# One key tile per head from GpSimd to VectorE, and the row maxima turned by TensorE into ScalarE's hands, in a decoder layer's two attentions

## The reference

```python
x = layernorm(x + self_attention(x))          # 16 heads of 32; ALiBi bias, even heads look back, odd heads ahead
x = layernorm(x + cross_attention(x, context, mask))   # 16 heads of 32; mask[b, 0, q, k] == 0 gives -1e9
x = layernorm(x + feed_forward(x))            # quantised gate/up/down, inner width 1536
# attention, per head: softmax(q @ k.T / sqrt(32) + bias) @ v
```

## Time and profile before

| | us |
|---|---|
| median of three runs | 3442.01 |
| the profiled execution | 3449.42 |
| its span in the trace | 3447.6 |

### The profile page before, as it was taken

The page is one execution under the profiler, slowest core; times in us unless marked ns, Lnnn a source line. Parts: engine busy times, 40 slices in busy tenths (PEclk is TensorE's granted clock), DMA queues, the critical chain, the costliest instruction groups (busy, mean ns, idle before and its releaser), DMA issues. The chain is left out here.

```text
span 3447.6 us, 79793 instructions
## 1 busy us (share of the span) xinstructions
PE 2725.7 (79%) x24128; PEld 1463.9 (42%) x24128; DVE 2539.6 (74%) x4873; ACT 1712.4 (50%) x3083; POOL 2054.8 (60%) x1542
## 2 busy tenths in 40 slices
PE   6888568888886777999999999950999899500999
PEld 3444235555553432555555555530444333200444
DVE  7777667777775666888888888848334599795776
ACT  2344247666664223656665666530233466575433
POOL 2344479898987215999999999973200366532000
PEclk9999879898988887999999999975999999755999
DMA  7999933333435542122121131146533577578332
GB/s 250 289 303 312 259 106 124 116 122 118 128 123 160 182 159 90 41 72 67 47 80 57 43 87 49 41 129 238 193 119 134 174 246 260 194 241 357 121 122 79
DMA packets 339805, 519.79 MB, mean 151 GB/s; under 512 B 36097, under 2 KB 168961, under 8 KB 339714
## 3 DMA queue, kind: packets, MB, share of 16 engines
q1 hardware_dynamic: 331426, 500.87, 45.1%
q0 software_dynamic: 2752, 9.44, 0.8%
q10 hardware_dynamic: 5536, 8.40, 0.6%
HBM read 279.47 MB, written 202.64 MB: 140 GB/s over the span
## 5 line engine op out<-in xcount | busy, mean ns | idle before, releaser
L1038 POOL TENSOR_TENSOR cross_plo<-cross_p 128x1024 f16<-128x1024 f32 x512 | 959.9, 1912 | 83.9 <-ACT cross_p L891 83.9
L891 ACT ACTIVATE cross_p<-cross_st 128x512 f32<-128x512 f32 x1024 | 556.1, 595 | 374.9 <-PE cross_st L832 374.9
L948 DVE CUSTOM_DVE_ANT_0 cross_junk<-cross_sc,cross_mb 128x1024 bf16<-128x1024 f32 x512 | 614.9, 1219 | 113.2 <-PE cross_sc L795 107.9
L1038 POOL TENSOR_TENSOR self_plo<-self_p 128x1024 f16<-128x1024 f32 (+7 forms) x512 | 571.5, 1148 | 71.8 <-ACT self_p L891 68.1
L891 ACT ACTIVATE self_p<-self_st,self_strip 128x512 f32<-128x512 f32 (+3 forms) x768 | 418.6, 582 | 253.5 <-PE self_st L830 224.1
L948 DVE CUSTOM_DVE_ANT_0 self_junk<-self_sc,self_strip 128x1024 bf16<-128x1024 f32 (+7 forms) x512 | 373.8, 755 | 128.1 <-PE self_sc L795 121.8
L827 PE MATMUL cross_st<-cross_qa,cross_ka 97*128 97x512 f16 x1024 | 390.5, 381 | 1.9 <-ACT cross_p L891 1.9
L832 PE MATMUL cross_st<-cross_nm,idbig 128*128 128x512 f16 x1024 | 390.3, 381 | 0.0
L795 PE MATMUL cross_sc<-cross_ka,cross_qa 96*128 96x512 f16 x1024 | 311.9, 387 | 67.4 <-DVE cross_qmax L948 50.3
L1853 PE MATMUL d_acc<-wd_hi,d_oh 128*128 128x512 f16 x384 | 146.8, 382 | 209.3 <-DVE d_ol L1891 209.3
L852 PEld LDWEIGHTS cross_o<-cross_vh,cross_p 128*128 128x128 bf16 x4096 | 270.5, 97 | 77.2 <-issue 23.2
(11 more groups left out here) (233 smaller groups left out, 6136.2 us busy)
## 6 DMA issues: line engine op xcount, KB each, us to landing
self_strip<-self_strips SPq DMA_DIRECT2D x68, 520.0 KB, 3.0
v_g<-scr_gate SPq DMA_DIRECT2D x97, 256.0 KB, 3.6
scr_gate<-gt_y SPq DMA_DIRECT2D x96, 256.0 KB, 2.0
scr_h<-v_h SPq DMA_DIRECT2D x96, 256.0 KB, 2.2
j_h<-scr_h SPq DMA_DIRECT2D x48, 512.0 KB, 4.5
m<-in_mask_Bx1xSxS_ik SPq DMA_DIRECT2D x34, 512.0 KB, 7.8
d_o<-scr_o SPq DMA_DIRECT2D x9, 1536.0 KB
scr_up<-v_y SPq DMA_DIRECT2D x48, 256.0 KB, 3.3
```

The lines of the kernel that those rows point to most:

```text
L891: nc.scalar.activation(p32[u % NPR][:, q0:q1], stp[cc % 2][:, 0:q1 - q0], ACT.Exp, bias=bias, scale=SM).then_inc(expd, 1)
L948: nc.vector.tensor_tensor_reduce(junk[slot % 2][:, 0:w], sc[slot % 2][:, 0:w], bias, 1.0, -3e38, ALU.add, ALU.max, qmax[n % 2][:, qt:qt + ...
L1038: nc.gpsimd.tensor_tensor(plo[u % NPR][:, q], p32[u % NPR][:, q], high[:, q], ALU.subtract).then_inc(lo_g, 1)
```

## The change

The row maxima leave VectorE except for the maxima themselves. `mneg` and VectorE's `max_row` are gone. TensorE transposes `qmax` itself, into a chunk of `stp` ahead of the key scores of a head's tile 4 (`TURN`), and ScalarE multiplies it with -1/BIG into `mrow`. `sc` is then used by scores alone. In the self attention the position term that was part of `mneg` comes in as one more row of `qa` (row 97), made once, stored in DRAM and loaded by one more DMA a head; the key scores there multiply 98 rows instead of 97.

VectorE makes `plo` of one key tile in eight: tile 4 in the cross attention (1024 columns), tile 5 in the self attention (384 columns). It does so in its own order after the maxima of step t for tile t+3. That is the head's step 1 in the cross attention, and step 2 in the self attention, between the maxima and `scale`.

```diff
-def slot_of_scores(u):
-    return u + max(0, (u - 2) // UH)
...
+        def on_vector(u):
+            return u % UH == (5 if causal else 4)
...
                 def load_max(i, n):
-                    sp.wait_ge(taken, i * (HB * (UH + 1)) + max_slot(i, n) + 3)
+                    sp.wait_ge(row_made, i * HB + n + 1)
...
+                def load_place(i, n):
+                    slot = (i * HB + n) % H
+                    sp.dma_start(qa[n % NQK][3 * HD + 1:3 * HD + 2, :], place_dram[ds(slot, 1), :]).then_inc(place_in[n % NQK], 16)
...
-                    nc.tensor.transpose(sc[slot % 2][0:ST, 0:P], mneg[n % 2][:], c["idf"][:]).then_inc(scored, 1)
+                def turn_max(i, n, cc, last=False):
+                    pe.wait_ge(taken, i * (HB * UH) + (min(n + 1, HB) if last else n + 1) * UH + 2)
+                    pe.wait_ge(expd, i * CS + cc + 1)
+                    nc.tensor.transpose(stp[cc % 2][0:ST, 0:P], qmax[n % 2][:], c["idf"][:]).then_inc(chunked, 1)
...
-                        lhs = ka[j][0:3 * HD + 1, kt * P:(kt + 1) * P]
+                        lhs = ka[j][0:KR, kt * P:(kt + 1) * P]
...
                 def step(i, t, last):
                     ahead(i, t + SLEAD, last)
+                    late_max(i, t + ELEAD, last)
                     if within(last, t + ELEAD):
                         key_scores(i, t + ELEAD)
                     values(i, t)
...
+                def max_row(i, n, cc):
+                    act.wait_ge(chunked, i * CS + cc + 1)
+                    act.wait_ge(mrow_in[n % NQK], (i + n // NQK) * 16)
+                    nc.scalar.mul(mrow[n % NQK][:], stp[cc % 2][0:ST, 0:P], -1.0 / BIG).then_inc(expd, 1)
+                    act.wait_ge(expd, i * CS + cc + 3)
+                    act.sem_inc(row_made, 1)
...
-                    if at == UH - 1:
-                        dve.wait_ge(taken, done + 3)
-                        if causal:
-                            nc.vector.scalar_tensor_tensor(out=mneg[n % 2][:], in0=qmax[n % 2][:], scalar=-1.0 / BIG,
-                                                           in1=strip[n % NQK][:, S + ST:SW], op0=ALU.mult, op1=ALU.add).then_inc(negated, 1)
-                        else:
-                            nc.vector.tensor_scalar(mneg[n % 2][:], qmax[n % 2][:], -1.0 / BIG, None, ALU.mult).then_inc(negated, 1)
-
-                def max_row(i, n, slot):
-                    dve.wait_ge(scored, i * (HB * (UH + 1)) + slot + 1)
-                    dve.wait_ge(mrow_in[n % NQK], (i + n // NQK) * 16)
-                    nc.vector.tensor_copy(mrow[n % NQK][:], sc[slot % 2][0:ST, 0:P]).then_inc(taken, 1)
...
+                def low(i, u):
+                    n, at, kt = keys_of(u)
+                    if not on_vector(u):
+                        return
+                    dve.wait_ge(expd, i * CS + chunks_by(u) + 2)
+                    q = slice(*query_range(n, kt))
+                    high = p32[u % NPR][:].bitcast(BF16).rearrange("p (q h) -> p q h", h=2)[:, :, 1]
+                    nc.vector.tensor_tensor(plo[u % NPR][:, q], p32[u % NPR][:, q], high[:, q], ALU.subtract).then_inc(lo_v, 1)
...
                     ahead(i, t + SLEAD, last)
+                    if within(last, t + ELEAD - 3):
+                        low(i, t + ELEAD - 3)
                     n = to_finish(i, t, SCALE)
                     if n is not None:
                         scale(i, n)
```

More of the change, by code:

```diff
@@ L601, in attention_phase @@
             tri = [sb(f"tri{j}", [P, P], F16) for j in range(2)]
-            SW = S + 2 * ST
+            SW = S + ST
+            place = sb("place", [H, S], F16)
+            at_q, own, slope = sb("at_q", [H, S], F32), sb("own", [P, H], F32), sb("slope", [P, 1], F32)
+            placed, place_out, place_in = sem("placed"), sem("place_out"), [sem(f"place_in{j}") for j in range(NQK)]
             strips = sb("strips", [P, H, SW], F32)
@@ L636, in chunks_before, with chunks_by, turn_before @@
         def chunks_before(u):
-            return sum(len(chunks(m // UH, keys_of(m)[2])) for m in range(u))
-        CS = chunks_before(HB * UH)
+            return 1 + sum(len(chunks(m // UH, keys_of(m)[2])) for m in range(u)) + u // UH + (u % UH >= TURN)
+        def chunks_by(u):
+            return chunks_before(u) + len(chunks(u // UH, keys_of(u)[2]))
+        def turn_before(u):
+            return chunks_before(u) - 1
+        CS = chunks_before(HB * UH) - 1
+        KR = 3 * HD + (2 if causal else 1)
         def steps(eng, prologue, step):
@@ L657, in to_finish, with lows_before @@
             return n - 1 if k == late and (n > 0 or not isinstance(i, int) or i > 0) else None
-        def max_slot(i, n):
-            return slot_of_max(n) if not isinstance(i, int) else slot_of_max(n + i * HB) - (UH + 1) * HB * i
+        def on_vector(u):
+            return u % UH == (5 if causal else 4)
+        def lows_before(u, vector):
+            return sum(on_vector(m) == vector for m in range(u))
+        LV, LG = lows_before(HB * UH, True), lows_before(HB * UH, False)
         def within(last, u):
@@ L707, in step @@
                         store(i - 1)
-                    if k == 0 and within(last, (n + 1) * UH):
-                        load_max(i, n + 1)
+                    if k == UH - 1 and within(last, (n + 2) * UH):
+                        load_max(i, n + 2)
                     if k == 1 and n > 0 or t == 1:
@@ L747, in _ @@
                 if causal:
-                    sp.wait_ge(ready, NQK + 2 * H)
+                    sp.wait_ge(ready, NQK + H)
                     for n in range(NQK):
@@ L751, in _ @@
                         load_strip(0, n)
+                if causal:
+                    sp.wait_ge(placed, 3)
+                    sp.dma_start(place_dram, place[:]).then_inc(place_out, 16)
+                    sp.wait_ge(place_out, 16)
+                    for n in range(NQK):
+                        load_place(0, n)
                 load_max(0, 0)
+                load_max(0, 1)
                 if causal:
@@ L858, in _ @@
                 if causal:
-                    pe.wait_ge(made, 9 + H)
+                    pe.wait_ge(made, 10 + H)
                 pe.wait_ge(ready, NQK)
@@ L893, in exps, with late_max @@
                         cc += 1
+                def max_row(i, n, cc):
[4 more added lines that the diff above has]
+                    act.sem_inc(row_made, 1)
+                def late_max(i, u, last):
+                    if u % UH == TURN and within(last, u):
+                        max_row(i, u // UH + 1, turn_before(u))
                 def prologue():
+                    max_row(0, 0, 0)
                     for u in range(ELEAD):
+                        late_max(0, u, False)
                         exps(0, u)
                 def step(i, t, last):
+                    late_max(i, t + ELEAD, last)
                     if within(last, t + ELEAD):
@@ L1022, in _ @@
                                        allow_small_or_imprecise_dtypes=True).then_inc(made, 1)
-                    pool.wait_ge(made, 5 + H)
+                    pool.wait_ge(made, 6 + H)
                     for j, sign in enumerate((-1, 1)):
```

86 lines of the change are left out of this document (46 added, 40 removed).

## The result

| | before | after |
|---|---|---|
| median of six runs, us | 3437.99 (3432.27 to 3444.65) | 3507.88 (3487.48 to 3515.95) |
| span of the profiled execution, us | 3447.6 | 3513.8 |
| self attention, first scores to last values | 658.4 | 779.9 |
| cross attention, first scores to last values | 992.2 | 942.7 |

The ratio is 1.0205, with a 95% interval of 1.0173 to 1.0236: slower by 70 us, where +82 was forecast. By the spans it is +66.2: +121 in the self attention, -49.5 in the cross attention, -6 in the rest. In the changed kernel scores are L818, the transpose L826, key scores L852 to L857, the exps L923, the copy of the maxima on ScalarE L931, maxima L998, VectorE's subtraction L1012, `ost` L1032, GpSimd's subtraction L1085. On SP the head loads are L685, the values L689, the maxima row L693, the place row L699, the strip L704, the store L709.

A forecast was written before the change was run, and what follows sets the result against it. GpSimd bounds the cross attention, TensorE just behind; the self attention follows a scores-maxima-scores loop. Cross -50 plus self +132 gives +82 us: 3531 on the profiled execution, 3524 against the median; range over the cases 3375 to 3607.

The forecast's parts named there:

- Forecast -50: Cross attention: a head falls from 15.0 to 14.2 us, GpSimd and TensorE level; over 62 heads -50 us.
- The wait that VectorE might have had for the port: Cross attention: VectorE's subtraction waits 0 to 1.86 us for the port; TensorE could stall 0 to 1.3, taken as none.
- The chain: Self attention: subtraction takes the gap, `ost` waits out the 1024 tile, maxima of 640 columns start late; +1.7 us a head.
- the 10.95 forecast: Self attention: a head's time in us if all heads are short; +70 us over 62 heads.
- All long: Self attention: every head has a stretch at TensorE's lower clock, 11.95 us a head; +132 us over 62 heads.
- The 0.4 us a head that the freed buffer of scores was to give: Self attention: without `mneg` and the transpose's wait, tile 2's scores come at 708.6 instead of 709.01; -0.4 us a head.
- The margin: Self attention: `ost` misses the gap ahead of GpSimd's 1024 tile by 0.3 us, in both heads read.
- Rival 1: Self attention: `ost` doesn't meet the 1024 tile; -25 to -5 us there, 3367 to 3387 in all; chance 0.18.
- Rival 2: Cross attention gains nothing: the subtraction's wait stalls TensorE, a head stays at 15.0 us; 3574; chance 0.1.
- Rival 3: Self attention: TensorE's clock has two low stretches a head instead of one; +65 us, 3589; chance 0.07.
- Rival 4: The change doesn't relieve GpSimd, as VectorE's work also blocks it; counted in the sum, 1.0 of 1.86 coming back; no chance given.
- SP's queue: Maxima row's DMA, issued behind the head loads of step 5: costs nothing, or 0.3 us a head if it lands late.

The follow-up runs named there:

- 5: Changed kernel with no VectorE subtraction in either attention, so the row maxima's part of the change alone: 3422.98 us, 0.9940.
- 4: Changed kernel with GpSimd making all key tiles of the self attention, cross attention as changed: 3377.13 us, 0.9798.
- 6: Kernel before with only VectorE's subtraction added for the same tiles; mneg, transpose and copy as before: 3623.06 us, 1.0531.
- 8: Changed kernel with the self attention's subtraction two steps earlier, in step 0, still for tile 5: 3374.58 us, 0.9802.
- 1: Changed kernel with `ost` ahead of the subtraction in the same step of the self attention: 3423.19 us, 0.9932.
- 2: Changed kernel with the self attention's reciprocal and `ost` moved from step 2 to step 4, the store as much later: 3374.59 us, 0.9785.
- 3: Changed kernel with VectorE subtracting only 64 of tile 5's 384 columns in the self attention, GpSimd the other 320: 3470.62 us, 1.0077.
- 7: Changed kernel with SP's store two steps later, behind the head loads, in both attentions: 3522.76 us, 1.0232.
- 9: Changed kernel with the self attention's subtraction in step 0 and the store two steps later: 3341.28 us, 0.9731.
- 10: Changed kernel with GpSimd making all key tiles of the self attention and the store two steps later: 3345.41 us, 0.9743.

## Why the prediction was right

**The parts.** By ratios to the kernel before: the rows alone -0.0060 (5), the cross attention's subtraction on top -0.0142 (4 against 5, about -49 us), the self attention's subtraction in step 2 on top +0.0407 (the changed kernel against 4, about +140 us). That these make +0.0205 is so by construction; the check is that the traces give the same: -49.5 us in the cross attention, and +121 in the self attention against -0.0060 + 0.0407, some +119 us.

**Cross attention: right, for the reason given.** Forecast -50, measured -49.5. The subtraction takes 1.6 us with its wait, holds GpSimd's next tile 1.0 us as taken, and that tile lasts 2.88 where 2.9 was named. TensorE's wait for the maxima of scores is gone from the list. The step of the scores around the transpose (1813.66 to 1815.69) is 2.03 us instead of 1.75, so a head is 8 x 1.745 + 0.29 = 14.25, with 14.2 forecast. The one number off is GpSimd's share, 96% and not over 97. The wait that VectorE might have had for the port, up to 1.86 us, was about 0.5, and TensorE didn't stall for it. What the prediction didn't say, and 5 and 6 show, is that neither half pays alone in a cross head: the two limits, at 15.0 and 15.0, had both to move. The prediction had read both (GpSimd 15.0, TensorE 14.0 plus one wait) without drawing that conclusion.

The port rule of the Trainium skill ("SBUF — State Buffer", section "Who interferes with whom"), by which the pair of ports is held for the whole instruction, agrees with the 1.0 us hold here.

**Self attention: the mechanism right, its size 11 us too large.** The chain was foretold row by row: subtraction in the gap, `ost` behind the 1024 tile (1.79 us; forecast 1.7), the maxima of 640 late, 1.91 us of idle TensorE ahead of tile 0's scores. The subtraction by itself lasts 0.55 us (8), not the 0.45 taken from rows 7, which only moves `ost` further behind the tile's start. A head at the full clock takes 11.0 to 11.1 against the 10.95 forecast. Experiments 1 to 4 and 8 tell it from the rivals of the study: moving either instruction takes it away, shrinking the subtraction hardly does. The term that was mis-sized is the clock. "All long", 11.95 a head, would have been +132; the mean is 11.76, +121. Of this (11.0 - 9.2) x 62 = 112 is the delay, and only about 9 what low stretches and the few short heads add to what low stretches cost before. The forecast had one stretch in every head. Of nine heads in a row (697.5 to 803.8 us) three have a clock of 1.00, two 0.85 and 0.88, and four 0.62 to 0.72, which is more than one stretch of 3 us (0.68 over 12.2 us). That the clock's part came out so near is luck: the heads without a stretch and those with more than one nearly cancel.

The 0.4 us a head that the freed buffer of scores was to give did come with the rows alone (9.82 to 9.45 in 5), but not for the reason given, or not for it alone: the clock from 500 to 1000 us rose from 0.90 to 0.98 there. By an estimate, that is 1.6 us a head less at the lower level, and at the price in the earlier trace rows, 1.1 us for 3 us, some 0.5 us: all of the gain.

**The margin was mis-sized.** The prediction had `ost` asking 0.3 us after the gap closed, from sums of short durations. In the head shown it asks 777.09 - 776.62 = 0.5 us after the 1024 tile's start, in others 0.2 (598.48 against 598.30); experiment 1, though, is decided by 0.02 against 0.08 us. The answer for the changed kernel held at both margins, but that for a swap of two lines was not to be had from such sums: both expectations of it missed.

**Rival 1** held in six heads, nearly all of them heads that a late maxima row puts into the other order (7). Its price, 0.1 to 0.4 us a head below the 9.82 of before, is borne out where `ost` is short in nearly all heads: 9.70 (2), 9.54 (4), 9.43 (8). Those six heads show no such gain, since most have the late row's wait on top. **Rival 2** didn't come; a cross head is 14.25. **Rival 3** came in part: the clock of the phase is 0.81, under the 0.83 named, and some heads have more than one low stretch. Read as (1 - clock) x 2 of the phase, the time at the lower level grew from about 158 us (0.88) to about 296 (0.81), more than the phase did, yet its cost grew by only about the 9 us above. The rule cited from the Trainium skill for it ("TensorE: Matmul & The Clock Gate", section "HAM oscillation — how this bites in real kernels"), idle gaps that return the kernel to the lower clock again and again, agrees in direction: pauses of 1.9 us a head with 0.82 from 500 to 1000 us, none of them with 1.00 (9). **Rival 4** is in the sum, 1.0 of 1.86.

**The weakest step was SP's queue.** "Nothing, or 0.3 us a head if it lands late" was said of the maxima row behind the head loads. In the changed kernel it is 6.6 us in 500 to 1060, covered by the larger pause. Once that pause is gone, it is what decides one head in four, by up to 3.2 us. Moving the store, and nothing else, takes the ratio from 0.9802 to 0.9731 (8 to 9) and from 0.9798 to 0.9743 (4 to 10), with intervals apart in both pairs: some 19 to 24 us, about a quarter of the 92 that 9 gains. The error was to look at the loads ahead of the row and not at what they wait for: the store, and through it `ost`.

**Left open.** How the 0.02 against 0.08 us of experiment 1 are settled in the hardware, and which pattern of pauses brings a second low stretch in one head and none in the next. TensorE's wait for the maxima alone doesn't tell: it is 24.2 us in 56 waits in the kernel before and 24.0 in 56 in experiment 2, at clocks of 0.90 and 0.94. Nothing here was made to tell.

## What to carry to other kernels

An instruction with two SBUF inputs put on VectorE beside a busy GpSimd costs by what GpSimd is running when it asks, and it takes the free moment from the next such instruction: before adding one, mark GpSimd's gaps and which of VectorE's instructions live in them. Where two engines are limits at the same pace, judge a change to either only together with the other. And after a wait is taken away, look at the DMA queue's order for the one that was hidden under it.

## What the chip showed beyond that

- 64 columns instead of 384 kept 1.2 of 1.9 us a head: the price of such an instruction is the GpSimd instruction behind which it puts itself or another one (1.8 us for `ost`), not its own 0.5.
- A VectorE instruction that waits goes ahead of GpSimd's *next* instruction every time that was looked at, even when the profile has that one started: 2.88 us for a 1024 tile behind the subtraction of 1024 columns, 2.31 behind 384 columns, 2.07 behind 256, against 1.89 undisturbed. In the profile, the hold stands in the duration of GpSimd's instruction, not as idle time.
- With pauses of 1.9 us a head TensorE's granted clock was 0.82 from 500 to 1000 us; without them (9) it was 1.00 over the same stretch, and 0.90 in the kernel before, whose waits for the maxima are 0.5 us at most. That the pauses are the cause is likely, not shown by itself: each run changes more than the pauses.
